# Two waits ahead of one weight's load in the SyncE queue of a perceiver block

## The reference, cut to what matters

```
# 1: causal self attention, cross attention over the context, two-layer network
x  = LN(x + self_attn(x, Wq1, Wk1, Wv1));  x = LN(x + cross_attn(x, ctx, Wq2, Wk2, Wv2))
x  = LN(x + relu(x @ fc1_w + fc1_b) @ fc2_w + fc2_b)
# 2: RWKV-7 time mix; the "time" axis is the two samples, so it has two steps
n4 = LN(x);  k, a, r, w, v, g = six mixes of n4, each @ its weight Wk, Wa, Wr, Ww, Wv, Wg
y  = group_norm(state @ r) + bonus;   z = (y * sigmoid(g)) @ Wo
h  = LN(n4 + z; norm_w, norm_b);  s = silu(h @ Wf + bf);  x = x + LN(s; lnf_w, lnf_b)
# 3: attention with routed value and output experts
n5 = LN(x);  q = n5 @ Wq;  k = n5 @ Wk;  gates and values from n5 @ [Ws, Wd, Wv]
x  = x + gated_attention(q, k, values) @ Wo
```

## Time and profile before

| | |
|---|---|
| profiled execution, its own time | 227.01 us |
| its span, first to last instruction | 225.3 us |
| median of the three runs | 226.76 us |
| PE busy | 216.2 us (96%) |
| DVE busy | 175.9 us (78%) |
| ACT busy | 112.9 us (50%) |
| POOL busy | 102.1 us (45%) |
| granted TensorE clock | 1.000 |
| HBM read | 43.27 MB, 194 GB/s over the span |

### The profile page before, as it was taken

How to read it: one execution, slowest core, us unless ns; L and a number is a source line. 1 busy time by engine, 2 the same in 40 slices (tenths; PEclk the granted TensorE clock), 3 DMA queues, 4 the chain that set the end, 5 groups by cost and what they waited for, 6 DMA issues and landing times.

```text
span 225.3 us, 3249 instructions
## 1 busy us (share of the span) xinstructions
PE 216.2 (96%) x1201; PEld 170.5 (76%) x1201; DVE 175.9 (78%) x320; ACT 112.9 (50%) x217; POOL 102.1 (45%) x90
## 2 busy tenths in 40 slices
PE   8999999999999999999898999998999899999995
PEld 8999889789888888888484757553566679798863
DVE  2056883877598988799678897699999899898971
ACT  2347521483689768935335287899412121246110
POOL 5016004760568336989330109979575218160000
PEclk9999999999999999999999999999999999999999
DMA  6999999069994499529690505707200000000002
GB/s 233 424 419 415 438 428 407 39 231 416 326 342 180 164 422 390 236 73 419 198 428 4 191 0 209 303 0 294 83 0 0 0 0 3 0 1 3 0 16 77
DMA packets 6784, 43.99 MB, mean 195 GB/s; under 512 B 881, under 2 KB 1393, under 8 KB 2033
## 3 DMA queue, kind: packets, MB, share of 16 engines
q1 hardware_dynamic: 6624, 43.66, 48.8%
q10 hardware_dynamic: 144, 0.13, 0.2%
HBM read 43.27 MB, written 0.52 MB: 194 GB/s over the span
## 4 chain that ended last, share of the span: by engine, by line
PE 76%; DVE 12%; DMA 5%; POOL 3%; issue 2%; ACT 2%; SPq 0%; DVEq 0%; POOLq 0%
PE psum L422 57%; PE psum L464 13%; DMA ring<-blocks 5%; PE psum L426 3%; ACT slots L1598 2%; PE psum L438 1%; DVE small L905 1%; POOL small L2049 1%; POOL small L2033 1%; PE psum L598 1%; DVE slots L915 1%; DVE slots L927 1%; DVE small L1159 1%; POOL slots L1936 1%; DVE small L1448 1%
## 5 line engine op out<-in xcount | busy, mean ns | idle before, releaser
L422 PE MATMUL psum<-ring_r,slots_r 128*128 128x512 f32 x360 | 88.7, 400 | 0.5 <-ACT slots_r L1598 0.3
L422 PEld LDWEIGHTS psum<-ring_r,slots_r 128*128 128x128 f32 x360 | 66.3, 188 | 19.0 <-ACT slots_r L1598 2.9
L1926 POOL TENSOR_TENSOR ring_r<-ring,ring_r 128x640 fp32r<-128x640 f32 x21 | 43.4, 2077 | 27.7 <-ACT ring_r L1598 27.7
L1598 ACT ACTIVATE slots<-psum 128x256 f32<-128x256 f32 (+4 forms) x48 | 20.4, 451 | 59.6 <-PE psum L422 22.1
L1598 ACT ACTIVATE ring_r<-ring 128x2048 fp32r<-128x2048 f32 x23 | 43.7, 1911 | 10.7 <-PE psum L422 9.3
L422 PE MATMUL psum<-ring,slots 128*128 128x512 f32 (+5 forms) x122 | 41.5, 483 | 2.0 <-issue 1.0
L933 DVE TENSOR_TENSOR ring_r<-ring,ring_r 128x1408 fp32r<-128x1408 f32 x21 | 35.8, 1708 | 3.0 <-ACT ring_r L1598 2.9
L464 PE MATMUL psum<-slots,ring 128*128 128x128 f32 x320 | 37.6, 277 | 0.1
L464 PEld LDWEIGHTS psum<-slots,ring 128*128 128x128 f32 x320 | 36.5, 192 | 0.9 <-ACT slots L1598 0.7
L422 PEld LDWEIGHTS psum<-ring,slots 128*128 128x128 f32 (+1 forms) x122 | 19.9, 190 | 17.1 <-issue 13.8
L1921 POOL TENSOR_TENSOR small<-small,mhalf 128x1 f32<-128x1 f32 x16 | 8.8, 549 | 43.9 <-DVE small L907 42.6
(11 more groups left out here) (179 smaller groups left out, 255.2 us busy)
## 6 DMA issues: line engine op xcount, KB each, us to landing
ring<-blocks SPq DMA_DIRECT2D x36, 1024.0 KB, 7.4
bc<-vecs SPq DMA_DIRECT2D x1, 3072.0 KB, 16.4
bc<-vecs SPq DMA_DIRECT2D x2, 512.0 KB, 15.5
bc<-vecs SPq DMA_DIRECT2D x1, 768.0 KB, 8.3
slots<-xin SPq DMA_DIRECT2D x1, 256.0 KB, 5.4
y<-slots SPq DMA_DIRECT2D x1, 256.0 KB, 2.1
y<-slots SPq DMA_DIRECT2D x2, 128.0 KB, 1.7
slots<-xin ACTq DMA_DIRECT2D x1, 128.0 KB, 2.7
```

The costliest lines, as they stand in the source:

```text
L422: return t.matmul(o_, l, r, start=first, stop=last)
L1598: return a.activation(o, x, func, **kw)
L1926: g.tensor_tensor(ring_r[:, p, CUT:], ring[:, p, CUT:], ring_r[:, high(name), CUT:], ALU.subtract).then_inc(*split_lowg.inc(name))
```

## The change

Two waits are put ahead of the load of block fk in SyncE's list: for product g of sample 0 and of sample 1. Nothing is taken out; the later waits for product v are on the same semaphores with lower values, so that `Waits` issues none for them. No other engine's list is touched.

```
@@ -395,6 +395,8 @@
             fetch("rr")
             fetch("fo")
             fetch("rf")
+            for b in range(2):
+                s.wait_ge(*prod[b].at("g"))
             fetch("fk")
             s.wait_ge(*normed[0].at("n4"))
             s.wait_ge(*normed[1].at("n4"))
```

## The result

| | before | after |
|---|---|---|
| median | 226.94 us (10 runs, 225.95 to 227.65) | 228.89 us (10 runs, 227.54 to 230.16) |
| ratio | | 1.0094, 95% interval 1.0064 to 1.0122 |
| profiled execution: time, span | 227.01, 225.3 us | 230.31, 228.6 us |
| mean granted TensorE clock of it | 1.000 | 0.993 |

The change makes the kernel 1.95 us slower. I had forecast 0.3 us. The measured median lies outside my range, 0.5 us above its upper end of 228.4. The ratio is not the quotient of the two medians, which is 1.0086; the same holds for the table of experiments.

What follows compares the result with a forecast made beforehand. Bound: the chain from ro(1) on TensorE through transposes, bias, rf(0), tanh and silu(0) to fg(0). Late vectors cost 0.3 us, moved traffic 0: 227.01 plus 0.3 is 227.3 profiled, 227.1 against the median; range 226.0 to 228.4.

Steps and rivals of the forecast that it cites:

- SyncE released 0.07 us after g(1), fk at 160.85, the vectors at 161.30: SyncE's queue: fk issued at 160.85 instead of 136.85, the vectors at 161.30 instead of 137.30.
- fk lands after 4.8 us: Start of the new burst: fk, now first, lands 4.8 us after issue, at 165.65.
- Who is late: Users of the delayed loads: only VectorE's norm_h(0) waits for the vectors, about 0.35 us; the others have 2.2 us or more.
- Both branches let 0.25 to 0.35 through: TensorE's transposes and bias, and VectorE's silu(0), have 0.1 to 0.3 us slack; 0.3 us taken as loss.
- fk 160.85 + 4.8 = 165.65; the vectors 165.65 + 1.85 = 167.5: New burst on SyncE's queue: vectors land at 167.5, 1.85 us behind fk, 0.25 us after norm_h(0)'s earlier start.
- I had this case as a rival, at 0.15: Vectors' landing: a straggling transfer adds 1.3 us, giving 228.3 us on the median; chance 0.15.
- the tails of f2 and fg: Earlier bursts: f2's tail of 1.3 us and fg's of 0.6, both on the last transfer of a burst.
- rf(0), 3.46 us from that point: TensorE from the bias through rf(0): duration kept at 3.46 us, only pushed by 0.25 to 0.3 us.
- The traffic mattered: Engines sped up by DMA traffic moving away, 225.9 us; chance of a gain above 0.5%: 0.05.
- Fully hidden: Vectors land by 167.25 or VectorE reaches line 915 later, so no loss, 226.8 us; chance 0.17.
- The landing at 167.1 by the Trainium skill's fit: Vectors' landing by 2.0 us plus bytes at 436 GB/s: 6.2 us for fk and vectors together, no delay.

Runs made afterwards that it cites:

- e1: Changed kernel with the two waits behind the three norm vectors instead of ahead of fk; 226.93 us against 226.40 before, ratio 1.0017.
- e5: Changed kernel with everything still behind the waits but the vectors first, then fk, fq, fg; 226.44 us against 226.96 before, ratio 0.9988.
- e2: Changed kernel with 64 satisfied waits added and four warm-up matmuls removed at TensorE's start; 228.96 us against 226.40 before, ratio 1.0123.
- e6: Changed kernel with the vectors one block further back: fk, fq, vectors, fg; 233.59 us against 227.08 before, ratio 1.0293.
- e7: Changed kernel with fq and fg held back until product ro of sample 0; 229.57 us against 227.08 before, ratio 1.0117.
- e9: The changed kernel run again unedited, for a second trace; 229.17 us against 227.08 for the kernel before, ratio 1.0087.
- e3: Kernel before with 64 satisfied waits added and four warm-up matmuls removed at TensorE's start; 228.66 us against 226.40 unshifted, ratio 1.0107.

## Why the prediction was wrong

- SyncE released 0.07 us after g(1), fk at 160.85, the vectors at 161.30: right (160.86 and 161.28).
- fk lands after 4.8 us: right.
- Who is late: right. Only the vectors, only on VectorE's line for `norm_w`; fg, fq, fk and GpSimd's additions cost nothing (e1, e5).
- "Both branches let 0.25 to 0.35 through", no idle time to catch up: right in kind, 1.69 us of delay became 1.70 on TensorE.
- **The step that failed**: "fk 160.85 + 4.8 = 165.65; the vectors 165.65 + 1.85 = 167.5". The 1.85 us came from a burst in which no instruction load fell. In the new place one does, and the last increment comes 1.27 us behind the fifteenth. The delay was therefore 1.69 us and not 0.35. e2 bears the rest of the sum out: without the load VectorE waits 0.42 us and the loss is 0.3 us in the medians, 0.5 in the profiles.
- I had this case as a rival, at 0.15, and held the tails of f2 and fg to belong to the last transfer of a burst. The trace of before had the answer. f2's fifteenth increment is at 108.53 and its sixteenth at 109.87, with an instruction load at 105.81; fg's are at 159.44 and 160.05, with a shorter load (0.31 us) at 158.39; the burst of the earlier trace rows had no load and no tail. And a load stood at 162.8 us, in the very stretch into which the change moves the burst. Asking for the queues in that window would have shown this pattern, though not every tail in the trace has a load (see the last section), and given the rival, 228.3 against 228.9 measured, a far larger chance.
- A second term was missing: "rf(0), 3.46 us from that point" takes the duration as fixed. It is 5.02 us where the clock falls. I looked for what is pushed and not at what an idle stretch of 1.4 us does to the engine behind it. In the medians this is the smaller term, since 15 of 23 executions kept their clock.
- "The traffic mattered": it asked for 0.5% of gain; e5's interval leaves at most 0.4%, e1's next to none. "Fully hidden": even without the load (e2) VectorE waits 0.42 us; with the vectors first in the burst (e5) it does not wait. The landing at 167.1 by the Trainium skill's fit ("DMA: Bandwidth & Descriptors", section "Anatomy of one DMA — SWDGE (gpsimd) path") was too early on SyncE's queue: even the burst without a load, e2, needed 6.8 us from the issue of fk (162.12) to the vectors (168.91), where the estimate from that page's fit, made for GpSimd's path, is 6.2.

The Trainium skill, "Runtime: NRT & Kernel Launch", section "Instruction fetch mechanics", calls the cost of crossing a 16 KiB boundary of the instructions "mostly hidden". For the engine that fetches, the trace here agrees: at the nine loads of q8 in the changed kernel TensorE has no idle stretch over 0.25 us, and those it has are ended by other engines. What is not hidden is the delay that the fetch gives to a data transfer under way, 1.27 us here.

## What to carry to other kernels

When a load is made later, work out the landing of everything that is queued behind it, and look at which other queues, instruction loads above all, are active in the stretch where the burst will now lie. A landing is the last of sixteen increments, so a bound on it has to hold for the slowest share and not for the mean rate. Put the small transfer with the nearest use first: the order alone takes the loss away here (e5). Where the forecast makes TensorE idle longer than it did before (here 1.4 us, where the longest earlier stretches of about 1.0 us had kept the full clock), put a term for the clock beside the sum, or give it filler work in the gap.

## What was not expected of the hardware

- The instruction load of 0.02 MB that falls beside this burst takes 0.91 to 0.98 us of one DMA engine (1.25 us in e2, where it runs ahead of the burst), and one of a transfer's sixteen increments falls 1.2 to 1.4 us behind, in all eight profiles in which the load fell into the burst (on the vectors in five of them, on fk in e5, on fq in e1 and e6). Transfers queued directly behind keep a lag of 1.0 to 1.4 us (0.1 us in e7, where fq was held back). That the lagging increment belongs to the engine that carried the load fits the packets of e7, but the trace does not name the engines.
- Not every tail needs a load. In e1 two blocks in a burst at 63 to 72 us have their sixteenth increment 2.3 and 2.2 us behind the fifteenth (67.03 and 72.41), with no instruction load between 56 and 73 us. In other profiles the same two blocks have anything from under 0.1 to 1.5 us. What makes these I did not follow.
- The load itself starts later beside the burst: with no data moving it started at 162.8 us, in the changed kernel at 165.56, with TensorE's list at the same point. In six of the eight profiles it starts within 0.1 us of fk's landing. That it was held up behind fk's packets fits this and is argued.
- After 1.4 to 1.5 us of idle TensorE three profiles (the changed kernel, e7 and e9) have a clock of 1.2 GHz instead of 2.4, from 1.3 to 1.8 us behind the idle stretch and for 3.4 us; in the changed kernel 8 of 23 executions have the lower mean clock. After 3.9 us of idle time (e6) it was at 0.50 when TensorE resumed, and stayed there for 6.8 us. With fills and 0.56 or 0.61 us left idle the mean clock is low in none of 13 executions, and the 0.98 us ahead of product g of sample 0 in the changed kernel's profile (from 152.1 us) have the full clock behind them.
- Waits that are already satisfied are not free. 64 of them at the start of TensorE's list held the first matmul until 4.51 us where it had started at 1.05, some 54 ns each. TensorE's timeline in e3:

```profile
4.51 3.32 PE L422 MATMUL psum<-ones 128*128 128x128 f32 x14 [4.51 <-issue]
```
